# A convolution and expert kernel: per-channel input transfers, look-ups moved behind the transposes, filter products moved forward

## The reference

```python
P = dtA[:, :, None] * jnp.arange(length)
Cs = Cc * (jnp.exp(dtA) - 1.0) / A
K = 2.0 * jnp.einsum('hn,hnl->hl', Cs, jnp.exp(P)).real          # the filters
...
y = irfft(rfft(u_m, 2L) * rfft(K, 2L))[..., :L] + u_m * D; y = y * mask
...
w = top-2 of softmax(y @ gate_w.T), made to sum to 1
h = silu(y @ g.T) * (y @ u.T)                                    # per expert
out = x + einsum('bei,hei,be->bh', h, d, w)
```

## Time and profile before

| | |
|---|---|
| median of 3 runs | 513.03 us (506.79 to 514.28) |
| the profiled execution | 512.6 us |
| its span, first to last instruction | 510.6 us |
| PE busy | 445.5 us, 87% |
| DVE, ACT, POOL busy | 38%, 19%, 35% |
| mean granted clock of PE | 0.968 |
| moved by DMA | 115.97 MB, mean 227 GB/s |

### The profile page before, as it was taken

One profiled execution on the slowest core, in us unless ns is written; L12 is line 12 of the kernel. 1 busy time (PEld: TensorE's weight loads), 2 busy tenths in 40 slices (PEclk: granted clock), 3 DMA queues, 4 the chain that ended last, 5 costly groups with the idle time before them and its releaser, 6 DMA issues.

```text
span 510.6 us, 8905 instructions
## 1 busy us (share of the span) xinstructions
PE 445.5 (87%) x2834; PEld 383.4 (75%) x2834; DVE 196.0 (38%) x512; ACT 98.3 (19%) x227; POOL 177.5 (35%) x217
## 2 busy tenths in 40 slices
PE   0459799999999999877789999999999999999991
PEld 0458799888899999877777877877877787777760
DVE  6905334343444422668313322332322223233330
ACT  4930000000001000020012222222222222222220
POOL 4263403222222200008564434344446324652222
PEclk9979899999999999995889999999999999999997
DMA  9956969888988889995547897989898687855440
GB/s 315 330 167 212 290 228 309 282 276 289 271 270 302 302 309 321 397 311 170 171 154 184 222 284 154 309 202 274 238 268 199 146 262 164 171 84 82 77 73 16
DMA packets 39769, 115.97 MB, mean 227 GB/s; under 512 B 8754, under 2 KB 17202, under 8 KB 39602
## 3 DMA queue, kind: packets, MB, share of 16 engines
q1 hardware_dynamic: 18418, 73.49, 43.3%
q0 software_dynamic: 12096, 33.58, 28.9%
q10 hardware_dynamic: 9216, 8.39, 5.0%
HBM read 93.63 MB, written 40.66 MB: 263 GB/s over the span
## 4 chain that ended last, share of the span: by engine, by line
PE 72%; DMA 11%; issue 9%; DVE 5%; ACT 1%; POOL 0%; ACTq 0%; POOLq 0%; DVEq 0%; SPq 0%
PE conv_ps L1058 25%; PE conv_ps L944 23%; PE conv_ps L1079 13%; PE turn_ps L1069 7%; DMA arena<-k_rows 5%; DMA k_rows<-k_sb 5%; PE turn_ps L955 1%; DVE tmp L627 1%; PE conv_ps L1086 1%; DMA out<-arena,from_row 1%; DVE mask_t L776 1%; PE k_bank L936 1%; PE turn_ps L964 1%; DVE angle L673 0%; DMA skip_row<-skip 0%
## 5 line engine op out<-in xcount | busy, mean ns | idle before, releaser
L944 PE MATMUL conv_ps<-arena 128*128 128x256 f32 (+7 forms) x1024 | 158.8, 312 | 14.3 <-DMA arena<-k_rows 9.3
L944 PEld LDWEIGHTS conv_ps<-arena 128*128 128x128 f32 x1024 | 150.6, 194 | 22.2 <-issue 13.5
L1058 PE MATMUL conv_ps<-arena,ys_t 128*128 x640 | 135.5, 362 | 9.8 <-issue 7.3
L1058 PEld LDWEIGHTS conv_ps<-arena,ys_t 128*128 128x128 f32 x640 | 117.7, 193 | 29.3 <-issue 27.6
L462 POOL DMA_INDIRECT out<-arena,from_row x40 | 62.9, 1572 | 133.6 <-DMA out<-arena,from_row 96.2
L1079 PE MATMUL conv_ps<-arena,hid_t 112*128 x160 | 75.4, 593 | 1.0 <-DVE hid_t L906 1.0
L732 DVE TENSOR_TENSOR arena<-conv_ps,mask_t 128x256 f32<-128x256 f32 x64 | 26.8, 423 | 93.7 <-PE conv_ps L944 92.9
L899 DVE TENSOR_TENSOR hid<-silu,conv_ps 128x112 f32<-128x112 f32 x40 | 10.9, 271 | 117.1 <-ACT silu L581 107.1
L911 DVE TENSOR_SCALAR arena<-conv_ps,slot_weight 128x512 f32<-128x512 f32 x40 | 30.0, 751 | 42.4 <-PE conv_ps L1079 41.4
L391 POOL TENSOR_TENSOR am<-wave,cs_re 128x128 f32<-128x128 f32 x16 | 6.4, 401 | 113.4 <-ACT wave L524 106.2
L1079 PEld LDWEIGHTS conv_ps<-arena,hid_t 112*128 112x128 f32 x160 | 27.2, 190 | 20.8 <-issue 20.8
(11 more groups left out here) (149 smaller groups left out, 369.1 us busy)
## 6 DMA issues: line engine op xcount, KB each, us to landing
arena<-k_rows SPq DMA_DIRECT2D x14, 2048.0 KB, 10.6
arena<-gu_t SPq DMA_DIRECT2D x16, 896.0 KB
arena<-x_time SPq DMA_DIRECT2D x16, 512.0 KB, 4.4
y_rows<-y_blk ACTq DMA_DIRECT2D x64, 128.0 KB, 7.0
arena<-d_t SPq DMA_DIRECT2D x16, 448.0 KB
arena<-k_rows SPq DMA_DIRECT2D x8, 512.0 KB, 5.8
out<-arena,from_row POOLq DMA_INDIRECT x44
out<-ys SPq DMA_DIRECT2D x1, 512.0 KB, 7.4
```

The costliest lines, as they stand in the source:

```text
L944: last = nc.tensor.matmul(conv_ps[:, h, d * B:C * B], toep[:, p, h, d * P:(d + 1) * P], u_t[:, p, h, 0:(C - d) * B], start=(d == 0), stop= ...
L1058: last = nc.tensor.matmul(gu_ps, ys_t[:, t % 2, c, :], flat[:, bass.ds(bufs[t] * WE + c * GU, GU)], start=(c == 0), stop=(c == C - 1))
```

## The change

It does five things.

1. SP takes the groups channel by channel. Each channel has its own input transfer (128 KB) and Toeplitz transfer (512 KB), issued when PE has finished the same channel of group g-2; both count on one semaphore per buffer and channel, for which PE waits before each channel.
2. `look_up(t+1)` stands behind the eight transposes of `turn(t+1)`, before `down(t-1)`.
3. On POOL, `fold`, `not_first` and the clearing of three `ys` buffers stand before the wait for the coefficients.
4. On ACT, `growth` of channels 8 to 63 is cut in two: 8 to 39 before the second sine, 40 to 63 behind it.
5. On PE, `products(1)` moves from behind channel 0 of group 0 into the `stay_awake` matmuls (14 before it, 7 behind it); `products(2)` takes its old place; `products(3)` stays.

```diff
@@ SP, for each group g
-                if g >= 2:
-                    sp.wait_ge(conv_done, (g - 1) * HG)
-                    sp.dma_start(u_t[:, p, :, :], x_time[:, g * HG:(g + 1) * HG, :]).then_inc(u_in[p], 16)
-
                 sp.wait_ge(k_stored[p], 16 * (i + 1))
-                if g < 2:
-                    for h in range(HG):
-                        sp.dma_start(toep[:, p, h, :], ...).then_inc(toep_first[p][h], 16)
-                else:
-                    sp.dma_start(toep[:, p, :, :], bass.AP(k_rows, g * HG * KROW, [[1, P], [KROW, HG], [1, L]])
-                                 ).then_inc(toep_in[p], 16)
+                for h in range(HG):
+                    if g >= 2:
+                        sp.wait_ge(conv_done, (g - 2) * HG + h + 1)
+                        sp.dma_start(u_t[:, p, h, :], x_time[:, g * HG + h, :]).then_inc(toep_in[p][h], 16)
+                    sp.dma_start(toep[:, p, h, :], bass.AP(k_rows, (g * HG + h) * KROW, [[1, P], [1, L]])
+                                 ).then_inc(toep_in[p][h], 16)
@@ POOL
             nc.gpsimd.tensor_tensor(tmp[:, 22, :], tmp[:, 22, :], tmp[:, 23, :], ALU.add).then_inc(square_made, 1)
+            # fold (three tensor_tensor), not_first (two memset), ys[:, 1:, :] (one memset) stand here now
             pool.wait_ge(coef_made, 2)
             pool.wait_ge(mag_made, 1)
             for p in range(2):
                 factors(p, p, True)
                 phases(2 + p, p, False)
-            # and no longer here
-            pool.wait_ge(mag_made, 2)
+            pool.wait_ge(mag_made, 3)
@@ ACT
             waves(0, 0, True)
-            growth(2 * HG, H)
+            growth(2 * HG, 10 * HG)
             waves(1, 1, True)
+            growth(10 * HG, H)
@@ PE
             def convolve(g, p, i, second=False):
-                pe.wait_ge(u_in[p], 16 * (i + 1))
-                pe.wait_ge(toep_in[p], 16 * i)
                 for h in range(HG):
+                    pe.wait_ge(toep_in[p][h], 32 * i + 16)
                     convolve_channel(g, h, p, False)
...
             products(0, 0, True)
-            stay_awake(21, turn_ps[:, 2, 0:P])
-            convolve_first(0, lambda: products(1, 1, False))
-            for g in range(2, 4):
-                products(g, g % 2, False)
+            stay_awake(14, turn_ps[:, 2, 0:P])
+            products(1, 1, False)
+            stay_awake(7, turn_ps[:, 2, 0:P])
+            convolve_first(0, lambda: products(2, 0, False))
+            products(3, 1, False)
             convolve_first(1, lambda: None)
...
-                    if c == 2 and t + 1 < hi:
-                        look_up(t + 1)
...
                     if t + 1 < hi:
                         turn(t + 1)
+                        look_up(t + 1)
                     if t > lo:
                         down(t - 1)
```

More of the change, by code:

```diff
@@ L204, in build @@
         k_stored = [sem(f"k_stored{i}") for i in range(2)]
-        toep_in = [sem(f"toep_in{i}") for i in range(2)]
-        toep_first = [[sem(f"toep_first{p}_{h}") for h in range(HG)] for p in range(2)]
+        toep_in = [[sem(f"toep_in{p}_{h}") for h in range(HG)] for p in range(2)]
         u_in = [sem(f"u_in{i}") for i in range(2)]
@@ L305, in _ @@
                              k_sb[:, p, :, :]).then_inc(k_stored[p], 16)
-                if g >= 2:
-                    sp.wait_ge(conv_done, (g - 1) * HG)
-                    sp.dma_start(u_t[:, p, :, :], x_time[:, g * HG:(g + 1) * HG, :]).then_inc(u_in[p], 16)
                 sp.wait_ge(k_stored[p], 16 * (i + 1))
-                if g < 2:
-                    for h in range(HG):
-                        sp.dma_start(toep[:, p, h, :], bass.AP(k_rows, (g * HG + h) * KROW, [[1, P], [1, L]])
-                                     ).then_inc(toep_first[p][h], 16)
-                else:
-                    sp.dma_start(toep[:, p, :, :], bass.AP(k_rows, g * HG * KROW, [[1, P], [KROW, HG], [1, L]])
-                                 ).then_inc(toep_in[p], 16)
+                for h in range(HG):
[4 more added lines that the diff above has]
+                                 ).then_inc(toep_in[p][h], 16)
             for e in range(3):
@@ L409, in _ @@
             nc.gpsimd.tensor_tensor(tmp[:, 22, :], tmp[:, 22, :], tmp[:, 23, :], ALU.add).then_inc(square_made, 1)
[L410 to L414, removed]
             link(nc.gpsimd.tensor_tensor(fold[:, :], ident[:, 0:E], ident[:, Q:Q + E], ALU.add))
@@ L421, in _ @@
             nc.gpsimd.memset(ys[:, 1:, :], 0.0).then_inc(ys_cleared, 1)
-            pool.wait_ge(mag_made, 2)
+            pool.wait_ge(coef_made, 2)
+            pool.wait_ge(mag_made, 1)
+            for p in range(2):
+                factors(p, p, True)
+                phases(2 + p, p, False)
+            pool.wait_ge(mag_made, 3)
             with pool.Fori(1, G // 2 - 1) as i:
@@ L970, in convolve_first @@
                 for h in range(HG):
-                    pe.wait_ge(toep_first[g][h], 16)
+                    pe.wait_ge(toep_in[g][h], 16)
                     convolve_channel(g, h, g, g == 0)
@@ L1050, in look_up, with gate_up @@
                 needs[t] = pe.value_load(tile_i[0:1, 1, t:t + 1], min_val=1, max_val=E)
-            def gate_up(t, hi):
+            def gate_up(t):
                 pe.wait_ge(weights_ready, needs[t])
@@ L1094, in tiles_of @@
                 for t in range(lo, hi):
-                    gate_up(t, hi)
+                    gate_up(t)
                     if t + 1 < hi:
                         turn(t + 1)
+                        look_up(t + 1)
                     if t > lo:
```

## The result

The changed kernel takes 495.7 us (median of 4, 494.9 to 498.8) against 512.8 for the kernel before (506.8 to 514.3): ratio 0.974, 95% interval [0.969, 0.980]. Forecast were 490 in a range of 484 to 500. The profiled execution of after took 496.27 us, with a span of 494.2 and a mean granted clock of 0.98.

The account below looks back on a forecast made before the run. PE, busy 87% of the span, was taken as the bound, so time is gained only where it waits. 512.6 - 10.3 (channel-wise transfers) - 0.9 (start) - 11.5 (experts) = 489.9, so 490 us; range 484 to 500.

Parts of the forecast that it names:

- Experts, -11.5: Expert stage: look-ups hidden behind PE's queue, 38 tiles at 5.73 us instead of 6.06; 12.4 us less small charges.
- My 0.5 for tiles with two late loads: Expert stage: 0.5 us deducted from the 12.4 us gain for tiles in which both register loads come late.
- Rival 2: Expert stage: cover only 0.87 us, so some 8 us lost instead of gained; 509 us, chance 0.06.
- Scatters: POOL's scatters in the expert stage: lag grows to about 12 us, within the buffers' limit; 0.4 us charged.
- Rival 1: Expert stage: POOL's scatter pace of 5.95 us becomes PE's, gaining 4.2 instead of 11.5; 497 us, chance 0.13.
- Channel-wise transfers, -10.3: Convolution: issuing channel by channel, up to 8 us earlier, removes PE's waits for Toeplitz transfers; 10.3 us gained.
- The 4.9 for group 2: Convolution: group 2's 3.25 us wait and its slow first channel (4.11 instead of 2.48) go.
- The 4.1 for five groups and 1.3 for the last two: Convolution: five groups go from 11.41 to 10.59 us each, and the last two lose late starts of 0.47 and 0.86.
- is issued 3.5 us after the end of group g-3: Convolution, SP's queue: filter store issued then, behind one last 512 KB piece, leaving 6 us of slack.
- Rival 4: Convolution: the filters' store comes late behind pieces and the slack is lost again; 500 us, chance 0.05.
- Start, -0.9: Between channel 3 and group 1: 1.4 us of products and waiting shrinks, one 0.3 us product stays; net 0.9 gained.
- Rival 3: Convolution: pieces pay their latency one behind the other, 23.2 us of transfer a group; 666 us, chance 0.04.

Follow-up runs that it names:

- six loads: The changed kernel with each look-up's two register loads done three times; 639.4 us in one execution.
- the store mid-way: The changed kernel with the filter store of group g+1 issued on SP ahead of group g's fourth channel's pieces; 487.3 us, ratio 0.957 to before.
- the start alone: The kernel before with only POOL's work forward, growth in two runs and kernel products moved; 509.2 us, ratio 0.998.

## Why the prediction was right in the whole and wrong in one half

**Experts, -11.5: right.** 38 tiles took 218.45 us, 5.75 each; 11.7 us won. The whole step held: queue far enough ahead (cover 2.8 us, where I had 2.4), loads hidden, no gap before `down` that PE's waits count. My 0.5 for tiles with two late loads was not needed. Rival 2, the gap only moves, is refuted by the position of the loads and by the run with them doubled. The nearest thing to it was seen only with six loads.

**Scatters.** The lag reached 10.5 us where I said up to 12, and PE never waited for it. But I had read one tile of before, with 2.8 us; the largest lag there was already 8.9, so it grew by 1.6 us and not by 9. Rival 1 fell. POOL's pace was not fixed at 5.95: between the third and the thirtieth scatter it was (437.31 - 281.06) / 27 = 5.79. It went down when PE's pace did, so it had been set in part by PE; I had treated it as POOL's own limit.

**Channel-wise transfers, -10.3: wrong; they gave about 1 in the profiled executions, and alone nothing that can be measured.** The three terms fared differently. The 4.9 for group 2 came, against the profile of before; the kernel with the look-up alone, whose convolution is the same as before's, lost only 0.2 us there by the same count, and before with its stores on ACT lost 6.4, so the size of this term differs from one execution to the next. The 4.1 for five groups and 1.3 for the last two did not come; in their place 3.8 were lost in this execution.

The step that failed is the sentence that the store "is issued 3.5 us after the end of group g-3", with only one 512 KB piece ahead of it, and so has 6 us of slack. I took the store's issue from the order of the old kernel, where nothing but one large transfer stands ahead of it. In the new order it stands behind the last of eight transfers, which themselves wait for the store before, all in one burst. The store's landing and the issues lie one behind the other on one queue; I charged each against PE's 10.59 us by itself. Both were also set too low. "Some 9 us after the end of g-3" is 5.5 us from the store's issue, and it took 7.0 at the median; the issues were to be 0.3 to 0.4 us each, and eight took 4.3. My own sizes add up to at most 9.5, which fits into 10.59; the measured 11.3 does not.

The trace of before held a warning that the prediction does not use. Its stores, issued behind one 2 MB transfer, landed after 8.3 us at the median, and 8.3 with eight issues of 0.3 to 0.4 us comes to 10.7 to 11.5:

```profile
DMA to landing us min/median/max: 2.1/8.3/10.3
```

Rival 4 named this mechanism, gave it 500 us and a chance of 0.05. It was what happened from group 4 on; 495.7 came out, because group 2's part was kept, and routing, first tile and tail gave 2.7 that I had not counted (the first `gate_up` ran at the full clock, 3.33 us instead of 6.33). The convolution missed by 9.2 us in the profiled execution, and a third of it was made up elsewhere; the range held the rest. That the total lies so near is partly luck: the first `gate_up` took 3.3 us with the look-up alone too, but 4.7 with the store mid-way and 6.3 with the transfers alone, edits that do not touch it.

**Start, -0.9: as forecast in place, too small to be measured.** Group 1 began at 45.62, forecast 45.7, and the added table loads cost nothing. That the start is so exact is chance too: in six other profiled kernels with the same start it began between 44.7 and 46.7, in three others with the old one between 46.5 and 49.3, as the low clock lasted for a shorter or a longer time. In the kernel with the start alone the clock hid it, as shown above. The warning that a full clock in channel 0 "only waits longer for `factors(2)`" was seen literally, 1.15 us in the store-mid version.

**The memset beside DVE, 0 to 2.66: the 0 was right.** In after it ran from 13.76 to 16.42, in the middle of DVE's chain, whose result `cs_im` came at 19.59 instead of 19.53. The Trainium skill, "SBUF — State Buffer", section "Who interferes with whom", limits the blocking by a GpSimd instruction that only writes to DVE's two-port modes. The trace agrees: 2.66 us of memset beside a dozen DVE instructions cost 0.06.

**Rival 3, pieces in series: fell.** Eight transfers issued within 4.3 us each landed in 6.6 us (Toeplitz) and 5.3 (input). The fixed 2.0 us that the Trainium skill gives for one transfer ("DMA: Bandwidth & Descriptors", section "Anatomy of one DMA — SWDGE (gpsimd) path") is stated there for transfers that GpSimd issues, and these are SP's. The trace shows no such serial cost on SP's queue: with the store elsewhere, eight transfers per group fit in 10.60 us.

## What to carry to other kernels

When a queue issues in order and waits for something that it has issued itself, write down its whole circle: the landing it waits for, plus every issue between that landing and the next request. If the sum exceeds the consumer's time per round, the circle is the bound, however much slack each transfer has alone. Take the landing from a transfer that stands behind as much as this one will. Here the split transfers gave slack only once the small store was issued when its data were ready: from another queue, or in the middle of the burst.

## What the hardware showed that was not expected

- A store of 16 KB took 7.0 us to land behind 2.5 MB on SP's queue, 6.0 us on ACT's queue, beside the stores of the results only, and 4.6 in the middle of a burst (medians). Another queue does not make it quick while the DMA engines are busy for 0.9 of the time; it only makes it early. With the waits gone (stores on ACT's queue) they were busy for 0.96 between 66 and 200 us, at 303 GB/s, while PE was busy for all of the 134 us: neither has room for a further gain there.
- A wait did not always cost the clock. The first channel after 2.71 and 3.10 us of idling ran at full speed (2.46 us); after 3.62 and 2.74 it took 4.01 and 3.93. In the convolution a wait of 2.60 us left the clock up (2.48) and one of 2.32 did not (4.15). At the start the low clock sometimes lasted into channel 1, for another 1.6 to 2.0 us. Length alone does not decide; what does was not tried.
- In the expert stage with six loads the first two gaps, of 1.2 and 2.3 us, left `down` at 1.98 us; the third, of 2.5, had 2.59 behind it, and after more tiles with such a gap in each it was 3.6.
- One register load in PE's queue takes 0.65 us with its check, and now and then 0.75 to 1.25 more; neither moving nor repeating it removed the late ones.
